# Reordered engine queues in a graph-attention stage, with two of four score sums handed from VectorE to ScalarE

## The reference, cut to what matters

```python
feat   = concatenate([x[src], edge_weights, x[dst]], axis=1)      # 64 + 16 + 64 = 144
h      = relu(feat @ W_att1.T + b_att1)                           # 144 wide
scores = (h @ W_att2.T + b_att2)[:, 0]                            # one number per edge
m      = segment_max(scores, src);  e = exp(scores - m[src])
alpha  = e / segment_sum(e, src)[src]
msg    = segment_sum(alpha[:, None] * lin_x[dst], src)            # then a GRU-like update of x
```

## Time and profile before

| what | value |
|---|---|
| median of three executions | 7888.26 us (7883.47 to 7888.82) |
| the profiled execution | 7885.51 us, its span 7883.6 us |
| busy share of the span: PE, DVE, ACT, POOL | 62%, 58%, 26%, 64% |
| attention stage | from about 5775 to 7750 us of the span, 468 ticks |

### The profile page before, as it was taken

The page is one execution under the profiler, slowest core; times in us unless marked ns, Lnnn a source line. Parts: engine busy times, 40 slices in busy tenths (PEclk is TensorE's granted clock), DMA queues, the critical chain, the costliest instruction groups (busy, mean ns, idle before and its releaser), DMA issues.

```text
span 7883.6 us, 169485 instructions
## 1 busy us (share of the span) xinstructions
PE 4875.0 (62%) x30913; PEld 3631.3 (46%) x30914; DVE 4538.2 (58%) x19982; ACT 2058.9 (26%) x5709; POOL 5047.4 (64%) x9951
## 2 busy tenths in 40 slices
PE   6333666566533475555555555555568888888887
PEld 3333333333333454444434444444446666666665
DVE  5666677677532482332323233232369999999997
ACT  4000000000000052222222222222235555555555
POOL 1666666666666446666666666666668878878886
PEclk9555555555555586667676666676689999999999
DMA  7222222222222224323222222222243443443443
GB/s 257 46 49 50 46 48 48 48 48 48 48 51 50 41 71 126 96 92 95 92 90 89 89 91 90 89 90 91 89 125 102 103 102 101 103 102 101 102 103 97
DMA packets 1160316, 670.13 MB, mean 85 GB/s; under 512 B 797187, under 2 KB 1060948, under 8 KB 1159396
## 3 DMA queue, kind: packets, MB, share of 16 engines
q1 hardware_dynamic: 1020628, 422.54, 21.8%
q0 software_dynamic: 137728, 243.98, 10.7%
q10 hardware_dynamic: 1888, 2.83, 0.1%
HBM read 371.08 MB, written 311.42 MB: 87 GB/s over the span
## 4 chain that ended last, share of the span: by engine, by line
another core or an unknown queue 15%; issue 15%; POOL 11%; PE 6%; DMA 4%; DVE 4%; ACT 3%; SPq 2%; DVEq 1%; POOLq 1%; ACTq 0%
PE banks L1402 4%; DMA wide<-rows_by_src 3%; POOL ring L875 2%; SPq L723 2%; ACT ring L1091 1%; ACT ring L1098 1%; POOL rows_by_src L841 1%; POOL ring L899 1%; DVE wide L2011 1%; POOL ring L893 1%; DVE wide L2016 1%; POOL ring L885 1%; DMA rows_by_src<-ring 1%; POOL ring L869 1%
## 5 line engine op out<-in xcount | busy, mean ns | idle before, releaser
L841 POOL DMA_INDIRECT rows_by_src<-ring x1760 | 1704.4, 968 | 1055.8 <-issue 517.8
L813 POOL DMA_INDIRECT wide<-msg_table,ring x1664 | 1576.5, 947 | 1062.8 <-issue 558.9
L1402 PE MATMUL banks<-wide,ring 128*128 x3520 | 1348.1, 513 | 938.1 <-ACT ring L1091 650.3
L1402 PEld LDWEIGHTS banks<-wide,ring 128*128 128x128 f32 x3520 | 793.7, 278 | 1192.2 <-issue 1150.2
L1316 PE MATMUL banks<-wide,ring 128*128 x3520 | 860.1, 426 | 680.0 <-DVE ring L1814 339.0
L1316 PEld LDWEIGHTS banks<-wide,ring 128*128 128x128 f32 x3520 | 784.9, 328 | 759.2 <-issue 758.7
L1098 ACT COPY ring<-banks 128x416 f32<-128x416 f32 x880 | 405.8, 518 | 1855.9 <-remote 1217.3
L1974 DVE COPY ring<-ring 128x4 f32<-128x4 f32 x440 | 81.8, 186 | 1353.0 <-DMA rows_by_src<-ring 1092.4
L1779 DVE TENSOR_TENSOR acc<-acc,banks 128x64 f32 x1760 | 389.2, 221 | 787.9 <-issue 269.1
L1443 PE MATMUL banks<-wide,ring 128*128 x5616 | 741.9, 282 | 2.2 <-ACT ring L1135 2.1
L1443 PEld LDWEIGHTS banks<-wide,ring 128*128 128x128 bf16 x5616 | 492.7, 98 | 160.5 <-issue 4.1
(11 more groups left out here) (334 smaller groups left out, 9797.6 us busy)
## 6 DMA issues: line engine op xcount, KB each, us to landing
wide<-rows_by_src SPq DMA_DIRECT2D x1872, 105.0 KB, 2.0
ring<-attr_turned SPq DMA_DIRECT2D x440, 128.0 KB
attr_turned<-ring SPq DMA_DIRECT2D x416, 96.0 KB
rows_by_src<-ring POOLq DMA_INDIRECT x1760
wide<-msg_table,ring POOLq DMA_INDIRECT x1664
ring<-attr_by_dst SPq DMA_DIRECT2D x208, 64.0 KB
attr_turned<-ring SPq DMA_DIRECT2D x208, 64.0 KB
attr_by_dst<-in_edge_attr_dram SPq DMA_DIRECT2D x1, 13281.2 KB
```

The source lines that it names most:

```text
L813: g.indirect_dma_start(out=A_g[:, b * GV + u, :], out_offset=None, in_=table[:, :], in_offset=bass.IndirectOffsetOnAxis(ap=A_idx[:, b * GV ...
L841: g.indirect_dma_start(out=rows_d[:, :], out_offset=bass.IndirectOffsetOnAxis(ap=B_pos[:, s, u:u + 1], axis=0), in_=B_row[:, s, u, :], in_ ...
L1402: mm(b, B_DT[:, t, u, :], qh[:, w, :].rearrange("p a k -> p (a k)"), start=True, stop=False)
```

## The change

Five things change, all in the attention stage:

1. DVE: the first two of the four scores become one operation over 2 x 144 elements without an accumulator (`terms`), which leaves the 288 terms in `C_V`. Scores 2 and 3 stay as they were. `c_raw` now counts 3 per step in place of 4.
2. ACT: two new operations per step sum these terms, an identity over 144 elements with ACT's accumulator into `C_raw`. They signal a new semaphore `c_sum`, on which ACT then waits before it copies the scores.
3. ACT's order: exp of the scores goes from the middle of the tick (stage 4) to its very front (stage 5), ahead of the sums; the one-hot complement goes ahead of the copy of PE's transposed parts.
4. POOL's order: the wait for `c_s` goes to the front of the tick; `C_W` goes from the tick's end (stage 4) to its front (stage 5), behind that wait; the score minus the maximum (`C_z`, `C_d`) goes from ahead of the running maximum to the end of the tick.
5. PE's products for the maximum go behind the linear part, and DVE's reduction of them goes behind the sums of the halves of h.

The new and changed lines, without those that only move:

```diff
 # POOL
             def tick(i, s, stages):
+                if 2 in stages:
+                    after_c(pool, c_s, *stages[2], incs=2)
+                if 5 in stages:
+                    t, j = stages[5]
+                    after_c(pool, c_p, t, j)
+                    after_c(pool, c_ag, t, j, 2)
+                    g.tensor_tensor(C_W[:, t % 2, :, :], C_V[:, t, :, H1:ROW_SRC],
+                                    per_group(C_p[:, t, :], HID + 1), ALU.mult).then_inc(c_W, 1)
...
 # ACT
             def tick(i, s, stages):
+                if 5 in stages:
+                    t, j = stages[5]
+                    after_c(act, c_d, t, j)
+                    after_c(act, c_W, t, j, CS)
+                    a.activation(C_p[:, t, :], C_d[:, t, :], ACT.Exp).then_inc(c_p, 1)
                 if 2 in stages:
                     t, j = stages[2]
-                    after_c(act, c_raw, t, j, incs=GV)
+                    after_c(act, c_raw, t, j, incs=PV + 1)
+                    for u in range(2):
+                        a.activation(C_V[:, t, u, 0:H1], C_V[:, t, u, 0:H1], ACT.Identity, accum_out=C_raw[:, t, u:u + 1]).then_inc(c_sum, 1)
+                    after_c(act, c_sum, t, j, incs=2)
                     after_c(act, c_pt, t, j, CS)
                     after_c(act, c_d, t, j, CS)
                     a.activation(C_parts[:, t, 0:GV], C_raw[:, t, :], ACT.Identity, bias=b2bc[:, :]).then_inc(c_s, 1)
...
 # PE
+                if 4 in stages:
+                    t, j = stages[4]
+                    after_c(pe, c_mn, t, j)
+                    after_c(pe, c_mg, t, j, 1)
+                    if 3 in stages:
+                        after_c(pe, c_new, *stages[3])
...
 # DVE
+                def terms(c):
+                    rows2 = C_V[:, t1, c, 0:H1]
+                    v.scalar_tensor_tensor(rows2, rows2, 0.0, w2bc[:, :].unsqueeze(1).to_broadcast([P, 2, H1]), ALU.max, ALU.mult).then_inc(c_raw, 1)
...
                     dve.wait_ge(c_add, (j1 * CS + t1) * 2 + 1)
-                    score(0)
-                    score(1)
+                    terms(slice(0, 2))
                     dve.wait_ge(c_add, (j1 * CS + t1) * 2 + 2)
                     score(2)
                     score(3)
```

More of the change, by code:

```diff
@@ L431, in build @@
         c_raw, c_s, c_mm = sem("c_raw"), sem("c_s"), sem("c_mm")
+        c_sum = sem("c_sum")
         kept = sem("kept")
@@ L865, in tick @@
                     sp_ = [C_parts[:, t, k * GV:(k + 1) * GV] for k in range(PARTS)]
-                    after_c(pool, c_s, t, j, incs=2)
                     after_c(pool, c_pt, t, j, CS)
@@ L870, in tick @@
                     g.tensor_tensor(sp_[2], C_r[:, t, :], sp_[1], ALU.subtract).then_inc(c_sp, 1)
-                if 4 in stages:
-                    t, j = stages[4]
-                    after_c(pool, c_mg, t, j)
-                    after_c(pool, c_p, t, j, CS)
-                    ch.link(g.tensor_tensor(C_z[:, t, :], C_s[:, t, :], C_mg[:, t, :], ALU.subtract))
-                    turn(pool, "pool")
-                    g.tensor_scalar(C_d[:, t, :], C_z[:, t, :], 0.0, None, ALU.min).then_inc(c_d, 1)
                 if 3 in stages:
@@ L896, in tick @@
                     t, j = stages[4]
-                    after_c(pool, c_p, t, j)
-                    after_c(pool, c_ag, t, j, 2)
-                    g.tensor_tensor(C_W[:, t % 2, :, :], C_V[:, t, :, H1:ROW_SRC],
-                                    per_group(C_p[:, t, :], HID + 1), ALU.mult).then_inc(c_W, 1)
-            run_ticks(pool, tick, 5, ch, CS * (2 + 1 + 4), CS, C_LOOPS)
+                    after_c(pool, c_mg, t, j)
+                    after_c(pool, c_p, t, j, CS)
+                    ch.link(g.tensor_tensor(C_z[:, t, :], C_s[:, t, :], C_mg[:, t, :], ALU.subtract))
+                    turn(pool, "pool")
+                    g.tensor_scalar(C_d[:, t, :], C_z[:, t, :], 0.0, None, ALU.min).then_inc(c_d, 1)
+            run_ticks(pool, tick, 6, ch, CS * (2 + 1 + 4), CS, C_LOOPS)
             def with_features(k):
@@ L1120, in tick @@
                     a.activation(C_cr[:, t, :], C_df[:, t, :], ACT.Exp).then_inc(c_cr, 1)
-                    after_c(act, c_d, t, j)
-                    after_c(act, c_W, t, j, CS)
-                    a.activation(C_p[:, t, :], C_d[:, t, :], ACT.Exp).then_inc(c_p, 1)
+                if 0 in stages:
+                    after_c(act, c_N, s, i)
+                    after_c(act, c_ag, s, i, CS)
+                    a.activation(C_S[:, s, :, :], C_N[:, s, :, :], ACT.Identity, bias=ones[:, 0:1], scale=-1.0).then_inc(c_S, 1)
                 if 2 in stages:
@@ L1129, in tick @@
                 if 0 in stages:
-                    after_c(act, c_N, s, i)
-                    after_c(act, c_ag, s, i, CS)
-                    a.activation(C_S[:, s, :, :], C_N[:, s, :, :], ACT.Identity, bias=ones[:, 0:1], scale=-1.0).then_inc(c_S, 1)
                     after_c(act, c_St, s, i)
@@ L1135, in tick @@
                     a.activation(C_STb[:, s, :, :], four(bank_b[0], P), ACT.Identity, bias=ones[:, 0:1], scale=-1.0).then_inc(c_STc, 1)
-            run_ticks(act, tick, 5, None, 0, CS, C_LOOPS)
+            run_ticks(act, tick, 6, None, 0, CS, C_LOOPS)
             act.wait_ge(n_ones, 1)
@@ L1417, in tick @@
                     r = regs(ENG.PE, wpair_of, j1 * (C_BODY // 2) + t1 * PV, N_WIN - 1, PV)
-                if 4 in stages:
-                    t, j = stages[4]
-                    after_c(pe, c_mn, t, j)
-                    after_c(pe, c_mg, t, j, 1)
-                    for u in range(GV):
-                        last = mm(bank[5][:, u * PARTS:(u + 1) * PARTS], C_STb[:, t, u, :], C_mp[:, t, u // 2, :], start=True, stop=True)
-                    last.then_inc(c_mm, 1)
                 if 3 in stages:
@@ L1445, in tick @@
                             last.then_inc(c_pre, 1)
+                if 4 in stages:
[4 more added lines that the diff above has]
+                        after_c(pe, c_new, *stages[3])
+                    for u in range(GV):
+                        last = mm(bank[5][:, u * PARTS:(u + 1) * PARTS], C_STb[:, t, u, :], C_mp[:, t, u // 2, :], start=True, stop=True)
+                    last.then_inc(c_mm, 1)
                 if 2 in stages:
```

11 lines of the change are left out of this document (6 added, 5 removed).

## The result

| | before | after |
|---|---|---|
| median of the runs | 7887.37 us (7883.47 to 7888.82) | 8452.01 us (8447.71 to 8460.92) |
| the profiled execution | 7885.5 us | 8460.92 us (span 8459.1) |
| a tick of the attention stage | 4.218 us | 5.450 us |

The changed kernel takes 1.0718 times as long (interval 1.07 to 1.0737). The prediction was 8445 us in 8180 to 8750. A tick is here the time between two of DVE's one-hots: the row that summarizes them gives their count and the start of the first and the last, and there are 467 gaps between 468.

What follows compares the result with a forecast made beforehand. DVE or the loop of loads through POOL was taken to hold the tick near 4.1 to 4.2 us. After: POOL 3.90 plus ACT 1.50 = 5.40, 1.185 more than 4.215, times 468 is 555 us: 8445 us, range 8180 to 8750.

Steps and rivals of the forecast that it cites:

- The mechanism: Attention stage: the tick becomes POOL's whole length plus ACT's five operations, without overlap, 5.40 us in place of 4.215.
- POOL's length: POOL's 13 operations in an attention tick: 3.71 us before, taken as 3.90 after, between 3.27 and 4.15.
- Both holds: POOL operations held by DVE: one by the one-hot, up to 0.13 us longer; one by the terms, some 0.1 longer.
- The first addition: On POOL: the one-hot starts right after `C_kl`, so the operation it holds is held up to 0.13 us longer.
- ACT's length: From POOL's `C_d` through ACT's exp, two sums and two copies back to POOL: 1.50 us, between 1.29 and about 2.0.
- DVE's saving worth nothing: DVE's scores save up to 0.45 us a tick, worth nothing because DVE waits for `C_kl` at ticks over 5 us.
- The rival in which a relieved DVE makes the kernel faster: DVE's queue sets the tick and ACT relieves it: about 4.1 us a tick, 7835 us; faster or no change 0.05.
- Loads hidden: SP's row loads have 3.88 us plus a whole tick before `C_kl` needs them: hidden by over 1 us.
- DVE waits over 1 us a tick ahead of L2058: Sign of being right: DVE waits that long ahead of its one-hot for POOL's L868.
- The rival of the clock: PE's clock falls too, two fifths at the lower level: 6.0 us a tick, 8720 us; 0.13 with both high ends.
- the signs of being wrong: POOL waiting under 1 us for ACT, DVE or PE over 85% busy, loads ending POOL's wait, or PE's waits and clock under 0.9.
- The whole: Sum for the attention stage: 3.90 + 1.50 = 5.40 us a tick, 555 us more over 468 ticks, 8445 us in all.

Runs made afterwards that it cites:

- E1: The changed kernel with all four scores back on DVE and no sums on ACT: 8088.78 us, ratio 1.0254 to the kernel before.
- E3: The changed kernel with POOL's wait for `c_s` back ahead of the splits, sums kept: 8065.6 us, ratio 1.0223 to the kernel before.
- E12: The changed kernel with ACT's two sums made twice: 8797.16 us, ratio 1.1157 to the kernel before.
- E10: The changed kernel with its terms made by two operations of 144 elements: 8512.68 us against 7978.36 for the kernel before, ratio 1.0664.
- E14: The changed kernel with all scores on DVE and the `c_s` wait back at the splits: 7984.87 us against 7991.84 before, ratio 0.9989.
- E2: The kernel before, its order kept, with terms on DVE and two sums on ACT: 8057.49 us, ratio 1.0213.
- E6: The changed kernel with 16 more unread products of 128 columns on PE each tick: 8448.4 us, ratio 1.0705 to the kernel before.

## Why the prediction was right, step by step

- **The mechanism** (POOL's length and ACT's, one after the other): right. It is named by the wait at L863, moved by E1 and E3 from two sides, and scaled by E12.
- **POOL's length:** 3.90 foreseen, 3.93 by tick less wait, in part by luck. Both holds are there: L877 at 570 ns, L892 at 393 against 194 to 202 of the operations that nothing holds. The second is the longer terms operation, estimated at 0.1 us and by E10 worth 0.08. But the 3.71 us to which the prediction added its 0.2 were those of one tick, and a short one: by tick less waits POOL's mean before was 3.83 (4.218 less 181.9 us in 465 ticks for ACT and the loads). The first addition, up to 0.13 for a one-hot that starts with POOL's operation, does not show: E1, which has the order without the terms, is at 3.85. A base some 0.1 too low and an addition some 0.1 too high cancelled.
- **ACT's length:** 1.50 foreseen, 1.46 in the tick shown, 1.52 as POOL's mean wait. By its parts, foreseen and read: exp after `C_d` 0.03 and 0.04, to the first sum 0.11 and 0.11, to the second 0.32 and 0.30, that one until written 0.42 and 0.41, signal 0.08 and 0.03, copies 0.46 and 0.48, to POOL 0.08 and 0.09. The guess for a readout that no row showed (0.19) was 0.19.
- **DVE's saving worth nothing:** right. E14 has DVE busy 177.4 of 200 us where before had 185.8, at the same tick; E2 has 162.3 and is slower. Most of the saving came from the order and not from the sums, as the last section shows. The rival in which a relieved DVE makes the kernel faster came true in none of the kernels with sums. Whether DVE, POOL or the loads set the tick of the kernel before is not shown.
- **Loads hidden:** right. L868, which must find them, shows 0.0 us of idle time in the group above; before, its like waited 65.3 us.
- **DVE waits over 1 us a tick ahead of L2058:** missed. It waits 273.9 / 459 = 0.60 us there, and 344.1 / 459 = 0.75 at L2017, for PE's L1474. The step forgot that PE's aggregation, which it named as held by `C_W`, is itself waited for by DVE ahead of the one-hot. That DVE idles over 1 us a tick was right, its place was not. Its busy share fell to 66%, where some 70% was foreseen. The place changes no term of the sum.
- **The rival of the clock:** its condition came in part, its price did not. The granted clock fell from 1.00 to 0.85, under the 0.9 that the prediction had named among the signs of being wrong, and PE went to 77% busy, where 66% was foreseen at the full clock. E6 shows no cost of this, which agrees with the sentence against the rival: the lower clock used up PE's slack first. Between the clock gate's two levels, 1.2 and 2.4 GHz, a mean of 0.85 is some 30% of the time at the lower one (0.7 x 1 + 0.3 x 0.5), less than the two fifths that the rival priced. The Trainium skill, "TensorE: Matmul & The Clock Gate" (HAM oscillation), describes such falls, and the time lost by them, for a PE that waits for DMAs longer than it computes between its waits. Here PE computes longer than it waits, the clock fell all the same, and the runs show no time lost by it.
- **The whole:** 8445 us against 8452. The 5.40 us of the sum against 5.450 by the profiled execution are 23 us apart over the stage; that the total is off by 7 is luck in part, since that execution was the slowest of the four.

## What to carry to other kernels

Put a wait directly ahead of the first instruction that needs it: on an engine that works its queue in order, everything behind the wait stands too, and here that cost 2.7% by itself and made the other half of the change twice as dear. A high busy share does not show that relief of that engine pays: every kernel here that took two of the sums off VectorE was slower than the one before, by 2.1% at the least. Look for who waits for the new owner's result, and add its whole duration where nothing stands between question and answer, as the doubled sums did here. Add up the tick as one engine's own work plus its waits for each of the others, and see which term an edit moves.
